# Probabilities turned by DMA transposes as fp16 pairs instead of by TensorE in fp32, and P·V as three fp16 products

## The reference, cut to what matters

```python
qg = q.reshape(B, N_KV_HEADS, g, T, hd)
scores = jnp.einsum('bgnqd,bgkd->bgnqk', qg, k) * scale
causal = jnp.tril(jnp.ones((T, T), bool))
scores = jnp.where(causal, scores, jnp.asarray(-1e+30, scores.dtype))
attn = jax.nn.softmax(scores, axis=-1)
out = jnp.einsum('bgnqk,bgkd->bgnqd', attn, v)
...
x = x + _L0_xattn_ref(_layernorm(x, axis=-1), ctx_512, ctx_512, ...)
x = x + _L0_ffn_ref(_layernorm(x, axis=-1), ...)
```

## Time and profile before

| | |
|---|---|
| median of 3 runs | 568.04 us (567.01 to 568.16) |
| the profiled execution: time, span | 565.63 us, 563.9 us |
| PE, DVE, ACT, POOL busy, share of the span | 91%, 63%, 47%, 37% |
| chain that ended last, by engine | PE 82%, POOL 6%, issue 4% |
| first up quarter starts | 110.48 us |
| one steady period | 28.11 us, 13 of them from 148.48 to 514.03 us |

### The profile page before, as it was taken

How to read it: one execution, slowest core, us unless ns; L and a number is a source line. 1 busy time by engine, 2 the same in 40 slices (tenths; PEclk the granted TensorE clock), 3 DMA queues, 4 the chain that set the end, 5 groups by cost and what they waited for, 6 DMA issues and landing times.

```text
span 563.9 us, 12246 instructions
## 1 busy us (share of the span) xinstructions
PE 514.3 (91%) x4968; PEld 366.7 (65%) x4968; DVE 356.2 (63%) x674; ACT 263.8 (47%) x819; POOL 205.8 (37%) x238
## 2 busy tenths in 40 slices
PE   0257888899999999999999999999999999999997
PEld 0124445475777676767676768686868686868683
DVE  1877636554586868686868686868686868473441
ACT  1457747646453535353545454545454545343110
POOL 2493754802515151525252525252525252222100
PEclk9999559799999999999999999999999999999999
DMA  8960703101203030303030303030303020200000
GB/s 175 293 165 6 240 26 108 37 3 33 59 10 80 11 80 11 81 11 81 11 80 12 80 13 78 11 82 10 80 17 75 11 58 10 57 2 20 2 21 19
DMA packets 59769, 31.87 MB, mean 57 GB/s; under 512 B 48288, under 2 KB 50608, under 8 KB 59664
## 3 DMA queue, kind: packets, MB, share of 16 engines
q1 hardware_dynamic: 56864, 30.58, 21.4%
q10 hardware_dynamic: 2768, 0.34, 0.5%
q0 software_dynamic: 80, 0.16, 0.1%
HBM read 16.39 MB, written 4.19 MB: 37 GB/s over the span
## 4 chain that ended last, share of the span: by engine, by line
PE 82%; POOL 6%; issue 4%; DMA 2%; SPq 2%; DVE 2%; ACT 2%; POOLq 0%; DVEq 0%
PE ff L680 31%; PE ff L695 29%; PE tb L661 7%; PE tb L543 4%; PE tb L650 3%; PE sb L642 2%; DMA big<-in_L_ffn_w_up_q 2%; POOL big L334 2%; PE ff L543 2%; POOL big L331 1%; POOL pr L360 1%; PE kxb L543 1%; PE ff L588 1%; PE ff L603 1%; ACT pr L477 1%
## 5 line engine op out<-in xcount | busy, mean ns | idle before, releaser
L680 PE MATMUL ff<-xnT_hi,wu_hi 128*128 128x128 f16 x1024 | 174.0, 219 | 2.0 <-ACT wd_lo L452 1.1
L360 POOL TENSOR_TENSOR pr<-pr,rinv 128x512 f32<-128x512 f32 x64 | 78.8, 1231 | 265.3 <-DVE rinv L824 265.3
L680 PE MATMUL ff<-xnT_hi,wu_lo 128*128 128x128 f16 x1024 | 173.9, 219 | 0.0
L680 PE MATMUL ff<-xnT_lo,wu_hi 128*128 128x128 f16 x1024 | 173.9, 219 | 0.0
L695 PE MATMUL ff<-wd_hi,x 128*128 128x512 f16 x512 | 152.4, 379 | 0.0
L680 PEld LDWEIGHTS ff<-xnT_hi,wu_hi 128*128 128x128 f16 x1024 | 100.1, 98 | 14.4 <-DVE z L843 11.7
L512 ACT ACTIVATE x<-z 128x512 f16<-128x512 f32 x64 | 40.4, 631 | 133.4 <-DVE z L843 133.4
L680 PEld LDWEIGHTS ff<-xnT_lo,wu_hi 128*128 128x128 f16 x1024 | 100.2, 98 | 0.3
L680 PEld LDWEIGHTS ff<-xnT_hi,wu_lo 128*128 128x128 f16 x1024 | 100.2, 98 | 0.0
L477 ACT ACTIVATE pr<-pr,nmax 128x128 f32<-128x128 f32 x256 | 98.8, 390 | 0.0
L695 PE MATMUL ff<-wd_lo,x 128*128 128x512 f16 x256 | 97.0, 379 | 0.0
(11 more groups left out here) (135 smaller groups left out, 687.2 us busy)
## 6 DMA issues: line engine op xcount, KB each, us to landing
xt<-in_x SPq DMA_DIRECT2D x16, 256.0 KB, 3.0
big<-in_L_ffn_w_up_q SPq DMA_DIRECT2D x4, 1024.0 KB, 13.9
big<-in_L_ffn_w_down_q SPq DMA_DIRECT2D x4, 1024.0 KB, 5.3
out<-y SPq DMA_DIRECT2D x16, 256.0 KB, 2.0
kvt<-in_ctx SPq DMA_DIRECT2D x16, 64.0 KB, 2.5
wd_lo<-in_L_xattn_w_out SPq DMA_DIRECT2D x1, 1024.0 KB, 13.7
wd_hi<-in_L_ffn_w_up_lora_b SPq DMA_DIRECT2D x3, 128.0 KB, 8.7
wd_hi<-in_L_xattn_q_norm_w SPq DMA_DIRECT2D x1, 256.0 KB, 6.6
```

What stands on the lines that cost most here:

```text
L360: pool.tensor_tensor(pr[:, m], pr[:, m], rinv[:, p, 4 * m:4 * m + 4].unsqueeze(2).broadcast_to([P, NG, P]), ALU.mult).then_inc(probs, 1)
L680: last = pe.matmul(bank[:, P * h:P * h + P], a[:, m, cols], b[:, p, m, :], start=(h == 0 and m == 0 and i == 0), stop=(m == KC - 1 and i = ...
```

## The change

It changes these things together:

- The row sums are first multiplied by 1/`P_TOP` (a new DVE instruction ahead of each reciprocal), so the probabilities come out scaled by 2^14.
- ACT rounds each head group's probabilities to fp16 (`p_high`), POOL subtracts to get the rest, also as fp16 (`p_low`, function `probabilities_low`), and both lie side by side in `p3`. SP issues a DMA transpose of 128x1024 fp16 for each head group, four in a batch. TensorE's turns and ACT's copies of them are gone.
- The values are scaled by the root of their sum of squares over the batch: TensorE multiplies `ssq` by a matrix of ones (function `turns`, R_VSUM), DVE forms `v_arg`, POOL takes two powers (`value_scales`), ACT and DVE write the high and low fp16 parts into `v3` (R_VSPLIT).
- P·V is three fp16 products of four matmuls each. The result is scaled back in ACT's and DVE's split of it (L467, L936 before); the weights of the projection carry 1/`P_TOP`.
- `p3` takes the fourth buffer of `stage`: the weight ring has three buffers, group 3 is no longer loaded at the start, and groups 3 to 7 are loaded in slots 4, 7, 10, 13 and 15 (before, 4 to 7 in slots 4, 7, 10 and 13).
- For batch 0 P·V, projection, residual and norm move one slot later; its up product stays in slot 18.

```diff
-R_PT = ((8, 15), (9, 16), (10, 17), (11, 18))
-R_PV, R_OSPLIT, R_PROJ, R_X1, R_POW2, R_NORM2, R_TURN2 = (12, 20), (13, 21), (13, 21), (14, 22), (14, 23), (15, 24), (16, 25)
+R_PSPLIT = ((8, 15), (9, 16), (10, 17), (11, 18))
+R_VSUM, R_VSPLIT = (9, 16), (10, 17)
+R_PV, R_OSPLIT, R_PROJ, R_X1, R_POW2, R_NORM2, R_TURN2 = (13, 20), (14, 21), (14, 21), (15, 22), (15, 23), (16, 24), (17, 25)
...
-RING = 4
+RING, W_RING = 4, 3
...
             def load_group(g):
-                if g >= 4:
-                    sp.wait_ge(w_turned, 4 * (g - 3))
+                if g >= W_RING:
+                    sp.wait_ge(w_turned, 4 * (g - W_RING + 1))
...
             load_group(2)
-            load_group(3)
             load_batch(2)
...
+                for m in range(NN):
+                    n = at(s, R_PSPLIT[m])
+                    if n is not None:
+                        sp.wait_ge(p_high, 4 * n + m + 1)
+                        sp.wait_ge(p_low, 4 * n + m + 1)
+                        if n > 0:
+                            sp.wait_ge(heads_out, n)
+                        sp.dma_start_transpose(pT[:, m], p3[:, m].rearrange("p g a t -> p (g a t)")).then_inc(p_turned, 16)
+                for g in range(W_RING, 8):
+                    if TILE_AT[4 * (g - W_RING) + 3] == s:
...
+            def probabilities_low(s):
+                for m in range(NN):
+                    n = at(s, R_PSPLIT[m])
+                    if n is not None:
+                        pool.wait_ge(p_high, 4 * n + m + 1)
+                        pool.tensor_tensor(p3[:, m, :, 1, :], pr[:, m], p3[:, m, :, 0, :], ALU.subtract).then_inc(p_low, 1)
+
+            def value_scales(s):
+                n = at(s, R_VSUM)
+                if n is not None:
+                    pool.wait_ge(v_arg_ready, n + 1)
+                    if n >= 2:
+                        pool.wait_ge(o_low, n - 1)
+                    pool.tensor_tensor(v_scales[:, n % 2, :], v_arg[:].broadcast_to([P, 2]), v_powers[:],
+                                       ALU.pow).then_inc(v_scaled, 1)
...
                 norm_and_residual(s)
+                value_scales(s)
+                probabilities_low(s)
...
+                    n = at(s, R_PSPLIT[m])
+                    if n is not None:
+                        act.wait_ge(probs, 4 * n + m + 1)
+                        if n > 0:
+                            act.wait_ge(p_turned, 16 * (4 * n + m - 3))
+                        act.activation(p3[:, m, :, 0, :], pr[:, m], ACT.Copy).then_inc(p_high, 1)
+                n = at(s, R_VSPLIT)
+                if n is not None:
+                    act.wait_ge(v_scaled, n + 1)
+                    if n > 0:
+                        act.wait_ge(heads_out, n)
+                    act.activation(v3[:, 0, :], kvt[:, n % RING, :], ACT.Identity,
+                                   scale=v_scales[:, n % 2, 0:1]).then_inc(v_high, 1)
...
-                    pe.wait_ge(probsT, 4 * n + 4)
-                    for g in range(NG):
-                        d = slice(HD * g, HD * g + HD)
-                        last = pe.matmul(tb[1][d, :], kvt[:, n % RING, d], prT[:, g].rearrange("p n t -> p (n t)"),
-                                         start=True, stop=True)
+                    pe.wait_ge(p_turned, 16 * (4 * n + 4))
+                    pe.wait_ge(v_high, n + 1)
+                    pe.wait_ge(v_low, n + 1)
+                    if n > 0:
+                        pe.wait_ge(o_low, n)
+                    for i, (a, b) in enumerate(((0, 0), (1, 0), (0, 1))):
+                        for g in range(NG):
+                            d = slice(HD * g, HD * g + HD)
+                            last = pe.matmul(tb[1][d, :], v3[:, a, d], pT[:, :, 2 * g + b, :],
+                                             start=(i == 0), stop=(i == 2))
```

106 lines of the change are left out of this document (63 added, 43 removed).

## The result

| | before | changed kernel |
|---|---|---|
| median of the runs | 568.10 us | 601.46 us (599.47 to 601.80, 4 runs) |
| ratio to before | | 1.0593, interval 1.056 to 1.0626 |
| span of the profiled execution | 563.9 us | 597.7 us |
| first up quarter | 110.48 us | 129.67 us |
| start of batch 1's up part (batches count from 0) | 148.48 us | 170.96 us |

The kernel is 5.9% slower; 573.2 us with a range to 588 was forecast. The table splits the 33.8 us of the span: 19.2 have been lost when the first up quarter begins, 3.3 more by batch 1, 11.4 in thirteen periods, nothing behind them. Most of the thirteen took 29.05 to 29.15 us, three took 29.34, 29.48 and 29.89, and the last two only 28.46 and 27.20.

What follows compares the result with a forecast made beforehand. It took PE to bound the steady period, with POOL's queue and the last transpose turning most of PE's gain into waits. +8.7 - 1.5 - 1.3 - 0.7 = +5.2 on 565.6 gave 570.8, for the median 573.2 us; range 552 to 588.

Steps and rivals of the forecast that it cites:

- What leaves PE: Steady period: probability turns 1.75 and shorter P·V 0.35 leave PE, product with ones adds 0.2; 1.9 us less.
- The rival of serial passes: P·V's three passes don't run side by side: P·V 2.6 us, total 600 us; chance 0.03.
- The up part starts at t = 12.9: Steady period, counted from the down quarters' start: POOL's queue and ACT's splits let the up product start at 12.9 us.
- P.V at t = 21.5 to 21.7, and 6.4 from there to the next t = 0: Steady period: P·V starts after scores (21.5) or last transpose (21.7, transpose 3.0); 6.4 us more make 28.1, taken as 28.0.
- The failed step of the steady sum: Steady period: each meeting of a POOL subtraction with DVE work was priced at 0.36 us lost by POOL.
- slow POOL: Rival for the steady period: 1.45 us per POOL subtraction, period 28.9, total 585 us; chance 0.15.
- Its second form: Clashes last as long as the whole DVE instruction: 0.3 to 0.9 us more a period, 577 to 585 us; shares chance 0.15.
- The weight preparation, +8.7, bounds 4 to 14: Start: late loads of groups 3 and 6 stall DVE; tile 12 6 us late, tile 24 8.7, first up quarter at 119.2.
- The 1.5 won up to 148 us: From the first up quarter to 148 us: PE is the bound, so the removed turns win 1.5 us.
- The 0.7 at the end: End of the kernel: no more keys on POOL for two periods and a shorter last P·V win 0.7 us.
- hidden stalls: Rival for the start: PE's order leaves 6 or 7 us that hide the weight stalls; cost 2, total 566.5 us; chance 0.10.
- a quick POOL: Rival for the steady period: subtraction 1.04 us and no clash, period 27.2, total 562 us; chance 0.17.

Runs made afterwards that it cites:

- e3: Changed kernel without POOL's four subtractions per batch (low parts of the probabilities stay zero): 574.68 us, ratio 1.0131.
- e9: e3 plus four POOL subtractions of constants, for which nobody waits, in the old places from batch 2 on: 593.10 us, ratio 1.0455.
- e12: e3 plus four POOL subtractions of constants, for which nobody waits, behind `t_cos` from batch 5 on: 576.39 us, ratio 1.0153.
- e1: Kernel before with only the weight ring of three buffers and its load rules: 585.42 us, ratio 1.0322.
- e8: Changed kernel with DVE's `oT_lo` ahead of the tiles' dequantisation in a slot: 595.18 us, ratio 1.0493.
- e4: Changed kernel with ACT's high `v` behind `xnT_hi` and DVE's low `v` behind `xnT_lo`: 595.78 us, ratio 1.0507.
- e5: Changed kernel with POOL's subtractions ahead of keys, `y` and value scales: 609.21 us, ratio 1.0735.
- e2: Changed kernel with the fourth weight buffer given back during the start: 587.26 us, ratio 1.0355.
- e15: Changed kernel with weight groups 3 to 7 loaded through ACT's queue, not SP's: 586.47 us, ratio 1.0336.
- e11: Changed kernel with the edits of e2, e8 and e4 and the subtractions moved from POOL to DVE: 563.18 us, ratio 0.9922.
- e16: e11 with three weight buffers and the loads through ACT's queue: 563.77 us, ratio 0.993.

## Why the prediction was wrong, by its own steps

The sum gave 570.8 us for the profiled execution, and it took 599.5. Of the 28.7 us between them 10.5 lie in the start (19.2 in place of 8.7), 4.8 in the stretch up to batch 1 (3.3 lost in place of 1.5 won) and the remaining 13.4 in the steady part with its end (11.4 lost in place of 2.0 won). Two steps failed: that PE's slack covers part of the second weight stall, and that a clash costs POOL 0.36 us and DVE nothing.

- **What leaves PE** (1.9 us a period): right in kind, 1.4 measured (28.11 to 26.72), 1.6 in e3 (26.47). The three passes ran side by side; P.V took 0.83, not 0.65, and the product with ones 0.28, not 0.2. The rival of serial passes is out.
- **The up part starts at t = 12.9**: measured 13.15 (PE waits for `xnT_lo`, 21.9 us in 13 waits). The queue of POOL was followed rightly: scales done at 10.6, as forecast, a subtraction 1.29 in the mean (1.26).
- **P.V at t = 21.5 to 21.7, and 6.4 from there to the next t = 0**: measured 22.35 and 6.70. The last subtractions ended sooner than forecast (17.7, not 18.7), but the transpose took 4.29, not 3.0. The median of all is 3.1; the last of this period, issued behind the queries' and two more of its own kind, is a late one, and so are the last ones in the four other periods in which PE waits for it (4.3 to 4.9). My bounds, 2.4 and 4.3, held the value and the middle was wrong.
- **The failed step of the steady sum** is in the sentences on the clash. I priced it as 0.36 us that POOL loses, and gave DVE nothing for it but the small multiplication. DVE loses more: in the steady stage `x2_lo` went from 684 to 949 ns in the mean, `t_sin` from 0.68 to 1.57 us, and the new 128x4 multiplication took 373 ns in place of 150. In the windows DVE's busy time is 4.1 us higher; 2.4 of that are the new instructions (the multiplications, partly held, and the low values), the rest is old ones that are held. So DVE became a third circle that I had not drawn, and six of eleven periods end through it. The forecast of 28.0 was 1.06 too low. 28.9, the "slow POOL" rival, came near the length of a period, but partly by luck: POOL's subtraction was not slow (1.29, not 1.45). Its second form, clashes as long as the whole instruction, was right in kind, but it is DVE that they made late. e3, e9 and e12 show that the subtractions make 2.0 us of the period, and by their place; e9's long periods put 0.9 of it on the held `t_sin`.
- **The weight preparation, +8.7, bounds 4 to 14**: 19.2. Each of the two stalls was foreseen in place and nearly in size (8.1 forecast and 8.86 measured for group 3; 100 and 102.2 for the landing of group 6; tile 12 late by 6 and by 8.3). Two things failed. First, I took the second as covered in part by slack that PE had, so that it added only 2.7 us, and put "the two stalls simply add up" at the edge, 14. In the changed kernel it adds 9.3, and e1 shows the same without the other changes, 9.8 + 10.0. Second, I let the projection of batch 0 run "after those scores", at 94, and did not see that `oT_lo` stands behind tile 24's dequantisation on DVE; it ran at 105.0 to 110.4, and from there my 13.6 us of POOL without a gap were 19.5 with gaps. e8 puts 4.3 us of the first up quarter on that. A third stall, group 5 behind three probability transposes (8.81 us of DVE's time), was missed too; the chain shows PE at work in that stretch, so it cost little by itself.
- **The 1.5 won up to 148 us** did not come: 3.3 us more were lost by batch 1. **The 0.7 at the end** did come, inside the thirteen periods: the last two were 0.6 and 1.9 us shorter than 29.06.
- **Of the rivals**, hidden stalls and a quick POOL are refuted. The clock stayed at 1.00 in twelve of the thirteen periods, as I had argued. The first one is the exception: after PE had stood 2.75 us ahead of 170.96, the granted clock was 0.59 from 172 to 176 us, and the period took 29.89. In e4 and e5 it fell after some waits of 1.9 to 3.2 us and not after others. A period in which it fell was 0.8 us longer than the usual one in the changed kernel, 1.0 to 1.6 in e5 and up to 4.5 in e4, the longer wait included.

What stays open: which part of the slots' new work makes the last 4 to 8 us of the start. With the loads mended the first up quarter is at 117.6 to 118.4 (e2, e15) and 114.9 to 115.5 with all edits (e11, e16), against 110.5; POOL's queue is on the chain from 64.9 to 79.2 us, but that was only read, not tested. Nor was it tested how the changed kernel's 2.0 us divide between the queue and the clash; 1.1 and 0.9 are read from e9's rows.

## What to carry to other kernels

Before a queue gets a new instruction that waits, list every transfer behind it; a load that had been early is late by the whole wait, and the ring size that forced it may be innocent (three buffers cost 17 us in SP's queue and nothing that can be measured in ACT's). An instruction's price on a shared engine depends on what stands behind it there and on what the other engine does at that moment: the same four subtractions cost 2.0 us a period in one place, 0.15 in another. When several circles have nearly the same length, walk all of them, the engines that are "only" 70% busy too, and add stalls unless a row shows the slack that covers them.

## What the runs showed of the hardware

The clash of POOL and DVE lasts until the other's instruction ends. In the changed kernel POOL and DVE show it side by side (first DVE, then POOL):
```profile
350.20 1.56 DVE L942 TENSOR_TENSOR t_sin<-xc,sw 128x512 f32<-128x512 f32 x1
351.69 1.75 DVE L905 SCALAR_TENSOR_TENSOR x<-z,x 128x512 f16<-128x512 f32 x1
```
```profile
348.76 2.46 POOL L391 TENSOR_TENSOR big<-pr,big 128x512 f16<-128x512 f32 x2
351.18 1.71 POOL L408 TENSOR_TENSOR t_cos<-xc,cw 128x512 f32<-128x512 f32 x1
```
`t_sin` (0.68 alone) ends 0.54 after the subtraction does, and `x2_lo` (0.68 alone) 0.55 after `t_cos` does: both did nearly all of their work only then, and `t_cos` (1.27 alone), which began during `t_sin`, ends 1.13 after it. Even a multiplication of 128x4 numbers (0.16 alone) takes 1.00 us in the changed kernel, 1.12 in e5 and 1.22 in e12 when it comes just after a POOL instruction began. This agrees with the Trainium skill, SBUF — State Buffer, section Who interferes with whom, which has the pair of ports held for a whole instruction. I had named 0.3 to 0.9 us more a period as the dearer case, 28.3 to 28.9; the period came out just beyond, at 29.06. The 0.36 us on which I had argued against it said nothing of the length of the hold: `q` had begun 0.17 us ahead of the probabilities at 282.12, which could meet only its last 0.49 us.

A transpose by DMA of eight blocks landed after 3.1 us in the median, 3.0 at the least, but after up to 5.2 in the changed kernel (5.5 in e4). In the five periods in which P.V waits for the last one, it is among the late ones.
